# Attention layer: five of a slot's sixteen pair sums folded by VectorE, three batches of ones products instead of four

## The chip, the core and the metric

One NeuronCore of one Trainium2 chip runs the whole program as one launch. The metric is device time in microseconds (us) from start to end of an execution. TensorE (PE) multiplies matrices into PSUM, VectorE (DVE), ScalarE (ACT) and GpSimd (POOL) work on tensors, and SyncE (SP) issues the DMAs. Each has a queue of instructions in a fixed order and waits on semaphores.

## What is computed

Two layers on a tensor of 4 images, 128 channels and 64x64 places. The change touches the first, self-attention over the 4096 places of an image with four heads of 32 channels, an output projection, the residual and a layer norm:

```python
Q = split_heads(x_flat @ Wq + bq); K = ...; V = ...
attn = softmax(einsum('bhnd,bhmd->bhnm', Q, K) * scale, axis=-1)
out = einsum('bhnm,bhmd->bhnd', attn, V)
y = (out.transpose(0, 2, 1, 3).reshape(B, H*W, C) @ Wo + bo) + x_flat
y = (y - mean(y)) / sqrt(var(y) + EPS) * gamma + beta
```

The second layer (a 3x3 convolution, a spectral mix and a Mamba scan) is the same in both kernels.

## The kernel before

**Slots and quads.** The attention runs in 128 slots: 4 images x 4 heads x 8 chunks of 512 queries. A slot has 32 key tiles of 128 keys, taken four at a time in 8 quads (`v` = 0 to 7). In each quad TensorE alternates four score products of queries by keys for the slot two ahead (`max_tile`, L369), of which VectorE takes the row maximum (L569), and four products of keys by queries for this slot (`exp_tile`, L376), of which ScalarE takes the exponential (L493). Behind these eight stands one batch of four products of exponentials and values (`attn_v`, L387), for the quad before; the four lie side by side in 32-column groups of the array. The trace shows each fp32 product as two records, so a batch is 8 records.

**The softmax denominator.** GpSimd adds the two halves of each pair of exponential tiles (L560, 16 pair sums of 128x512 a slot, in a ring `sums` of 8). TensorE then multiplies them by ones (`sum_exps`, L399), four pair sums a batch: a batch each for pairs 0 to 3, 4 to 7, 8 to 11 and 12 to 15, behind the exponentials of quads 2, 4, 6 and of quad 0 of the next slot. VectorE copies the result from PSUM (`read_den`, L580) in quad 0 of the next slot.

**Rings.** The score products that VectorE reads share three PSUM banks (`d` ring), those that ScalarE reads three others (`a` ring). A product can be issued only when the reader has released the bank of three products earlier. With four tiles in a quad, the fourth maximum product waits for VectorE's first maximum of the same quad. The exponentials go to `exps`, 4 buffers of one pair each.

**Around it.** After the first maximum of a slot's scores is joined (L574), TensorE turns it (`turn_max`, L405) in quad 1 and VectorE writes it as two fp32r rows (`shift_rows`, L586 and L588). In 24 of the slots the queries, keys and values of a chunk of the next image are projected: `project` in quads 1 and 2, ScalarE adds the bias into `full` (L507), VectorE makes its fp32r high part (`high`, L595, quads 2 and 4) and low part (`low`, L599, quads 3 and 5), both in `hilo`, and SyncE stores them. The 8 chunks of the first image are projected before slot 0, in a prologue. In 32 slots a chunk of the output is finished: `spread_den` in quad 4, `join_heads` (L431) in quad 5, `out_proj` in quad 6, `mean` in quad 7, `variance` in quad 1 of the next slot, with `normalise`, `add_x`, `centre` and `scale` on VectorE. ScalarE copies each slot's output into `heads_out`, which stays in SBUF for all four heads of an image (L501). The order is written out by loops over slot and quad, one loop for each engine.

Of the kernel before, what the change touches and what calls it, by code (L numbers as in the profile page):

```python
# [52 lines left out]
NS = B * HEADS * NCH  # L53
PRE = -NCH - 2
NF = B * NCH

# [73 lines left out]
def layer0(nc, x, w, z_ext, nb=B):  # L130
    qk_split = nc.dram_tensor("qk_split", [B, 2, 2, C, L], F32, kind="Internal").ap()
    v_dram = nc.dram_tensor("v_dram", [B, HEADS, 128, NT * D], F32, kind="Internal").ap()
    d_at, a_at = ring_positions()
    with ExitStack() as ctx:
# [22 lines left out]
        v_ring = sb("v_ring", [128, 2, NT, D])  # L157
        exps = sb("exps", [128, 4, 2 * CH])
        sums = sb("sums", [128, 8, CH])
        heads_out = sb("heads_out", [128, HEADS, L])  # L160
        mpart = sb("mpart", [128, 2, 4, NCH])
# [21 lines left out]
        with nc.Block() as block:  # L183
# [33 lines left out]
            def _(act):  # L217
# [6 lines left out]
                             "mneg_ready", "mrow_hi")]  # L224
        (made, split_ready, v_stored, recip_ready, squared, rstd_ready, scale_ready, z_ready, z_stored, f_in) = [
            sem(s) for s in ("made", "split_ready", "v_stored", "recip_ready", "squared", "rstd_ready", "scale_ready", "z_ready",
                             "z_stored", "f_in")]
        q_in = [sem(f"q_in{i}") for i in range(4)]
        k_piece = [sem(f"k_piece{i}") for i in range(NCH)]
        k_in, v_in, x_in, split_stored, mrow_stored, den_stored = [  # L230
            [sem(f"{s}{i}") for i in range(2)] for s in ("k_in", "v_in", "x_in", "split_stored", "mrow_stored", "den_stored")]
        MAX_BANK, EXP_BANK, OUT_BANK, DEN_BANK = 0, 3, 6, 7
# [17 lines left out]
        with nc.Block() as block:  # L250
            @block.sync
            def _(sp):
# [45 lines left out]
                def store_den(n):  # L298
# [6 lines left out]
                    sp.dma_start(denom[row:row + 4, half, :], den_parts[::D, n % 2, :]).then_inc(den_stored[n % 2], 16)  # L305

                def store_max(m):
# [10 lines left out]
                for n in range(PRE, NS + 2):  # L318
# [13 lines left out]
                    if 0 <= n - 1 < NS:  # L332
                        store_den(n - 1)
                    if 0 <= n + 1 < NS:
                        store_max(n + 1)
# [15 lines left out]
            def _(pe):  # L351
# [27 lines left out]
                def attn_v(n, v):  # L379
                    if v == 0:  # L380
                        if n:
                            pe.wait_ge(out_read, n)
                        if n % NCH == 0:
                            pe.wait_ge(v_in[n // NCH % 2], 16 * (n // NCH // 2 + 1))
                    pe.wait_ge(a_done, a_at["exp", n, 4 * v + 3] + 1)
                    for i in range(4):
                        ins = nc.tensor.matmul(ps[D * i:D * i + D, OUT_BANK, :], v_ring[:, n // NCH % 2, 4 * v + i, :],  # L387
                                               exps[:, (2 * v + i // 2) % 4, CH * (i % 2):CH * (i % 2) + CH],
                                               start=(v == 0), stop=(v == QUADS - 1))
                        if i % 2:  # L390
                            ins.then_inc(av_done, 1)

                def sum_exps(n, v):
                    if v == 1 and n:
                        pe.wait_ge(den_read, n)
                    pe.wait_ge(summed, n * PAIRS + 2 * v + 2)
                    for j in range(4):
                        u = 2 * v - 2 + j
                        nc.tensor.matmul(ps[D * j:D * j + D, DEN_BANK, :], ones_d[:, :], sums[:, u % 8, :],  # L399
                                         start=(v == 1), stop=(v == QUADS - 1)).then_inc(sum_used, 1)  # L400

# [25 lines left out]
                def join_heads(f):  # L427
                    pe.wait_ge(out_read, last_slot(f) + 1)
                    d_room(("join", f))
                    for h in range(HEADS):  # L430
                        ins = nc.tensor.matmul(d_bank(("join", f))[D * h:D * h + D, :], sel_o[:, :],  # L431
                                               heads_out[:, h, chunk(f % NCH)], start=True, stop=True)
                    ins.then_inc(d_ready, 1)
# [16 lines left out]
                for n in range(PRE, NS + 2):  # L450
                    p, f, g = projection_at(n), finish_at(n), finish_at(n - 1)
                    for v in range(QUADS):
# [24 lines left out]
                        if f is not None and v == 5:  # L477
                            join_heads(f)
                        if 0 <= m < NS and u % 2:
                            sum_exps(m, u)  # L480

            @block.scalar
            def _(act):
# [3 lines left out]
                def exp_tile(n, t):  # L487
                    u, half = t // 2, t % 2
                    ready(("exp", n, t))
                    if half == 0 and n * PAIRS + u >= 4:  # L490
                        act.wait_ge(av_done, n * PAIRS + u - 3)
                        act.wait_ge(summed, n * PAIRS + u - 3)
                    nc.scalar.activation(exps[:, u % 4, CH * half:CH * half + CH], a_bank(("exp", n, t)), ACT.Exp, scale=SCALE  # L493
                                         ).then_inc(a_done, 1)

                def read_out(n):
                    act.wait_ge(av_done, n * PAIRS + PAIRS)
                    f = batch_of(n) * NCH + n % NCH
                    if n // NCH % HEADS == 0 and f >= NCH:
                        act.wait_ge(d_done, d_at["join", f - NCH] + 1)  # L500
                    nc.scalar.copy(heads_out[:, n // NCH % HEADS, chunk(n % NCH)], ps[:, OUT_BANK, :]).then_inc(out_read, 1)  # L501

                def add_bias(p, i):
                    ready(("proj", p, i))
                    if p:
                        act.wait_ge(split_ready, 2 * p + i - 1)
                    nc.scalar.activation(full[:, i, :], a_bank(("proj", p, i)), ACT.Identity, bias=bias[:, i:i + 1]).then_inc(a_done, 1)  # L507

# [44 lines left out]
            @block.gpsimd  # L553
            def _(pool):
                for n in range(NS):
                    for u in range(PAIRS):
                        pool.wait_ge(a_done, a_at["exp", n, 2 * u + 1] + 1)
                        if n * PAIRS + u >= 8:
                            pool.wait_ge(sum_used, n * PAIRS + u - 7)
                        pool.tensor_tensor(sums[:, u % 8, :], exps[:, u % 4, 0:CH], exps[:, u % 4, CH:2 * CH], ALU.add).then_inc(summed, 1)  # L560

            @block.vector
            def _(dve):
# [12 lines left out]
                def read_den(n):  # L576
                    dve.wait_ge(sum_used, n * PAIRS + PAIRS)
                    if n >= 2:
# [11 lines left out]

                def high(p, i):
                    dve.wait_ge(a_done, a_at["proj", p, i] + 1)
                    if p >= 2:
                        dve.wait_ge(split_stored[p % 2], 64 * (p // 2))
                    nc.vector.tensor_copy(hilo[:, p % 2, i, 0, :], full[:, i, :]).then_inc(made, 1)  # L595

                def low(p, i):
                    dve.wait_ge(made, 2 * p + i + 1)
                    nc.vector.tensor_tensor(hilo[:, p % 2, i, 1, :], full[:, i, :], hilo[:, p % 2, i, 0, :].bitcast(F32), ALU.subtract  # L599
                                            ).then_inc(split_ready, 1)  # L600

# [33 lines left out]
                for n in range(PRE, NS + 2):  # L635
                    p, f, g = projection_at(n), finish_at(n), finish_at(n - 1)
                    for v in range(QUADS):
                        for m, t in max_tiles(n, v):
                            max_tile(m, t)
                        if v == 0:  # L640
                            if 0 <= n + 1 < NS:
                                join_max(n + 1)
                            if 0 <= n - 1 < NS:
                                read_den(n - 1)
                        if v == 1 and 0 <= n + 1 < NS:
                            shift_rows(n + 1)
                        if p is not None:
                            if v in (2, 4):
                                high(p, v // 2 - 1)
                            if v in (3, 5):  # L650
                                low(p, v // 2 - 1)
                            if v == 6:
# [667 lines left out]
```

## Time and profile before

| | us |
|---|---|
| median of 3 runs (lowest, highest) | 5985.74 (5984.24, 5988.39) |
| the profiled execution | 5988.07 |
| its span, first to last instruction | 5986.3 |
| TensorE busy | 5515.8 (92%) |
| VectorE busy | 4841.2 (81%) |
| GpSimd busy | 4207.8 (70%) |
| ScalarE busy | 3701.3 (62%) |

The profile gives each engine's busy time, groups of instructions by line, and a timeline in order of time. The first layer fills the first 3950 us or so. "Idle" in brackets is the time an engine stood still ahead of an instruction, with the engine that ended it. A busy TensorE is modelled from pipelined matmuls: it is in the distance between starts that its pace is read.

### The profile page before, as it was taken

What the parts mean: (1) busy time and instruction counts of PE and PEld (TensorE: products, weight loads), DVE (VectorE), ACT (ScalarE), POOL (GpSimd) and SP (SyncE); (2) the same over time, 40 slices, a digit from 0 to 9 for tenths busy, and PEclk for the clock granted to TensorE, in tenths of its full rate; (3) what the DMA queues carried; (4) which work ended last, traced back from release to release, by engine and by line L of the source; (5) the groups of instructions that cost most, each with busy time, mean ns of one, the idle gap of its engine ahead of it and who ended that gap; (6) DMA issues with size and microseconds to landing.
All of it is one profiled execution on the core that took longest, in us unless ns stands there. A gap on an engine that the chain in (4) does not pass through costs nothing. (4 is left out here: it accounts for less than half of the span.)

```text
span 5986.3 us, 84041 instructions
## 1 busy us (share of the span) xinstructions
PE 5515.8 (92%) x27184; PEld 2520.1 (42%) x27184; DVE 4841.2 (81%) x7122; ACT 3701.3 (62%) x7290; POOL 4207.8 (70%) x3213
## 2 busy tenths in 40 slices
PE   7999999999999999999999999968888878888887
PEld 4444444444444444444444444423333333333333
DVE  7777777777777777777777777639999999999999
ACT  3666666665666666666666666656666666666665
POOL 2767666677676677776667776638787887878787
PEclk8999999999999999999999999989999999999999
DMA  4011010110110101101010000024444444454444
GB/s 135 21 43 41 20 38 22 43 40 27 43 35 21 45 20 43 41 24 36 24 26 22 8 22 13 20 94 172 168 161 168 160 169 162 168 168 160 168 160 153
DMA packets 292503, 464.74 MB, mean 78 GB/s; under 512 B 72384, under 2 KB 95808, under 8 KB 290624
## 3 DMA queue, kind: packets, MB, share of 16 engines
q1 hardware_dynamic: 292064, 459.37, 23.6%
q8 instruction: 217, 3.56, 0.2%
q14 instruction: 222, 1.82, 0.1%
HBM read 381.41 MB, written 76.28 MB: 76 GB/s over the span
## 5 line engine op out<-in xcount | busy, mean ns | idle before, releaser
L560 POOL TENSOR_TENSOR sums<-exps 128x512 f32<-128x512 f32 x2048 | 2617.2, 1298 | 1313.2 <-ACT exps L493 1308.3
L569 DVE TENSOR_REDUCE mpart<-ps 128x1 f32<-128x512 f32 x4096 | 2541.6, 683 | 818.9 <-PE ps L369 818.9
L493 ACT ACTIVATE exps<-ps 128x512 f32<-128x512 f32 x4096 | 2127.9, 603 | 1404.0 <-PE ps L376 1403.6
L369 PE MATMUL ps<-k_st,q_ring 96*128 96x512 f32 x4096 | 1753.9, 429 | 17.3 <-DMA k_st<-qk_split 8.9
L1232 POOL TENSOR_TENSOR hc<-hh,c_rep 128x512 f32<-128x512 f32 x1024 | 1361.8, 1338 | 392.3 <-DVE hh L1195 391.9
L376 PE MATMUL ps<-q_ring,k_st 98*128 98x512 f32 x4096 | 1621.7, 397 | 4.0 <-ACT exps L493 3.6
L1195 DVE TENSOR_TENSOR_SCAN hh<-d_a,carry,ps 128x512 f32<-128x512 f32 x1024 | 1308.6, 1281 | 1.0
L369 PEld LDWEIGHTS ps<-k_st,q_ring 96*128 96x128 f32 x4096 | 775.1, 189 | 1063.4 <-DVE mpart L569 508.2
L387 PE MATMUL ps<-exps,v_ring 128*32 128x512 f32 x8192 | 1090.8, 605 | 0.0
L376 PEld LDWEIGHTS ps<-q_ring,k_st 98*128 98x128 f32 x4096 | 777.7, 190 | 148.4 <-ACT exps L493 17.3
L1021 PE MATMUL ps<-s_u,sel_g 128*128 128x512 f32 x1024 | 559.1, 549 | 199.0 <-DVE hh L1195 197.4
L1119 ACT ACTIVATE d_a<-d_a,a_neg 128x512 f32<-128x512 f32 x1024 | 730.8, 720 | 3.6 <-DMA d_a<-dt_dram 2.0
L1181 DVE TENSOR_TENSOR ps<-ps,b_rep 128x512 f32<-128x512 f32 x1024 | 700.8, 687 | 12.6 <-PE ps L1021 11.6
L1021 PEld LDWEIGHTS ps<-s_u,sel_g 128*128 128x128 f32 x1024 | 194.7, 191 | 870.0 <-DVE hh L1195 752.8
L399 PE MATMUL ps<-sums,ones_d 128*32 128x512 f32 x4096 | 533.1, 592 | 0.0
L1004 PE MATMUL ps<-hc,sel_y 128*32 128x512 f32 x2048 | 287.2, 633 | 183.6 <-DVE yt L1166 114.7
L387 PEld LDWEIGHTS ps<-exps,v_ring 128*32 128x32 f32 x8192 | 161.2, 108 | 416.9 <-ACT exps L493 361.2
L1112 ACT COPY carry<-hh 128x1 f32<-128x1 f32 x1024 | 186.7, 183 | 238.8 <-DVE hh L1195 238.5
L939 PE MATMUL ps<-za,wtap 128*128 128x512 f32 x528 | 266.0, 598 | 27.2 <-DMA stage_j<-z_ext 27.2
L986 PE MATMUL ps<-zp,wconv 128*128 128x512 f32 x576 | 290.0, 604 | 0.0
L399 PEld LDWEIGHTS ps<-sums,ones_d 128*32 128x32 f32 x4096 | 133.0, 110 | 306.6 <-issue 298.1
L1064 ACT CAST s_u<-ux 64x1024 fp32r<-64x1024 f32 x66 | 68.9, 1045 | 286.0 <-POOL ux L1223 285.2
(106 smaller groups left out, 3075.4 us busy)
## 6 DMA issues: line engine op xcount, KB each, us to landing
d_a<-dt_dram SPq DMA_DIRECT2D x1040, 256.0 KB
qk_split<-hilo SPq DMA_DIRECT2D x128, 256.0 KB, 2.3
q_ring<-qk_split SPq DMA_DIRECT2D x384, 64.0 KB, 2.0
k_st<-qk_split SPq DMA_DIRECT2D x45, 512.0 KB, 7.1
dt_dram<-dt SPq DMA_DIRECT2D x33, 512.0 KB, 2.8
za<-z_ext SPq DMA_DIRECT2D x33, 320.0 KB, 3.8
zp<-z_ext SPq DMA_DIRECT2D x32, 320.0 KB, 6.6
xc<-in_x SPq DMA_DIRECT2D x32, 256.0 KB, 3.0
```

Source lines behind the costliest of these rows:

```text
L369: nc.tensor.matmul(d_bank(("max", m, t)), q_ring[0:PARTS, m % 4, 128 * i:128 * i + 128], k_st[0:PARTS, g % 2, chunk(kc)], start=True, stop ...
L376: nc.tensor.matmul(a_bank(("exp", n, t)), k_st[0:SHIFT, n // NCH % 2, 128 * t:128 * t + 128], q_ring[0:SHIFT, n % 4, :], start=True, stop= ...
L387: ins = nc.tensor.matmul(ps[D * i:D * i + D, OUT_BANK, :], v_ring[:, n // NCH % 2, 4 * v + i, :], exps[:, (2 * v + i // 2) % 4, CH * (i % ...
L399: nc.tensor.matmul(ps[D * j:D * j + D, DEN_BANK, :], ones_d[:, :], sums[:, u % 8, :], start=(v == 1), stop=(v == QUADS - 1)).then_inc(sum_ ...
L493: nc.scalar.activation(exps[:, u % 4, CH * half:CH * half + CH], a_bank(("exp", n, t)), ACT.Exp, scale=SCALE).then_inc(a_done, 1)
L560: pool.tensor_tensor(sums[:, u % 8, :], exps[:, u % 4, 0:CH], exps[:, u % 4, CH:2 * CH], ALU.add).then_inc(summed, 1)
L569: nc.vector.tensor_reduce(mpart[:, m % 2, t % 4, t // 4:t // 4 + 1], d_bank(("max", m, t)), AX.X, ALU.max).then_inc(d_done, 1)
L1021: nc.tensor.matmul(ps[:, U_BANK + g % NU, :], sel_g[:, j, :], s_u[:, p, s, :], start=True, stop=True).then_inc(u_rep, 1)
L1119: nc.scalar.activation(d_a[:, g % NDA, :], d_a[:, g % NDA, :], ACT.Exp, scale=a_neg[:, s * 8 + j:s * 8 + j + 1]).then_inc(da_ready, 1)
L1181: nc.vector.tensor_tensor(bu, bu, b_rep[:, p, :], ALU.mult).then_inc(bu_ready, 1)
L1195: nc.vector.tensor_tensor_scan(hh[:, g % NHH, :], d_a[:, g % NDA, :], ps[:, U_BANK + g % NU, :], carry[:, it % STEPS, s * 8 + j:s * 8 + j ...
L1232: pool.tensor_tensor(hc[:, g % NHC, :], hh[:, g % NHH, :], c_rep[:, p, :], ALU.mult).then_inc(hc_ready, 1)
```

## The change

GpSimd writes the pair sums 0 to 4 of a slot to a new tile `held` of five buffers, not to the ring. VectorE adds these five into `held_sum` in four pieces of 128 columns, one behind the maxima of each of quads 3 to 6 (`join_held`): each piece reads 5 x 128 elements per partition in the order column by column, so that consecutive elements lie 512 elements apart, and writes 128. TensorE multiplies by ones in three batches: pairs 5 to 8 in quad 5, 9 to 12 in quad 7, and 13 to 15 with `held_sum` in quad 0 of the next slot.

It also moves other work. `exps` has 8 buffers, not 4. To make room, `heads_out` goes: ScalarE copies a slot's output to one of two buffers `out_sb`, SyncE stores each (256 KB) to DRAM (`store_out`) and, for each of the 32 finished chunks, loads the four heads back (1 MB, `load_heads`) before `join_heads`. The high part of a projection is written by a second ScalarE activation and the low part by GpSimd, so VectorE has neither. `read_den` moves from quad 0 to quad 1 behind `shift_rows`. `h_in`, `joined` and `out_stored` are semaphores.

```diff
+EXPS = 8
+HELD = 5
+ALONE = PAIRS - HELD
+UNITS = ALONE + 1
+def units(u):
+    return {4: (5, 6, 7, 8), 6: (9, 10, 11, 12), 7: (13, 14, 15, None)}.get(u, ())
...
 def store_out(n):
+    sp.wait_ge(out_read, n + 1)
+    f = batch_of(n) * NCH + n % NCH
+    if f >= 2 * NCH:
+        sp.wait_ge(h_in, 16 * (f - 2 * NCH + 1))
+    sp.dma_start(out_dram[...], out_sb[:, n % 2, :]).then_inc(out_stored[n % 2], 16)
+def load_heads(f):
+    if f:
+        sp.wait_ge(d_ready, d_at["join", f - 1] + 1)
+    sp.wait_ge(out_stored[f % 2], 16 * (last_slot(f) // 2 + 1))
+    sp.dma_start(heads_in[:, :, :], out_dram[...]).then_inc(h_in, 16)
...
 def sum_exps(n, v):
-    if v == 1 and n:
+    if v == 4 and n:
         pe.wait_ge(den_read, n)
-    pe.wait_ge(summed, n * PAIRS + 2 * v + 2)
-    for j in range(4):
+    pe.wait_ge(summed, n * PAIRS + (2 * v + 1 if v < 7 else PAIRS))
+    for j, u in enumerate(units(v)):
+        if u is None:
+            pe.wait_ge(joined, 4 * n + 4)
...
 def join_heads(f):
-    pe.wait_ge(out_read, last_slot(f) + 1)
+    pe.wait_ge(h_in, 16 * f + 16)
...
 # ScalarE, add_bias: a second activation
+    nc.scalar.activation(hilo[:, p % 2, i, 0, :], a_bank(("proj", p, i)), ACT.Identity, bias=bias[:, i:i + 1]).then_inc(a_done, 1)
 # GpSimd, behind the pair sums of quads 2 and 4
+def low(p, i):
+    pool.wait_ge(a_done, a_at["proj", p, i] + 1)
+    pool.tensor_tensor(hilo[:, p % 2, i, 1, :], full[:, i, :], hilo[:, p % 2, i, 0, :].bitcast(F32), ALU.subtract)
 # VectorE
+def join_held(n, i):
+    if i == 0:
+        dve.wait_ge(summed, n * PAIRS + HELD)
+        if n:
+            dve.wait_ge(sum_used, n * UNITS)
+    a = slice(128 * i, 128 * i + 128)
+    nc.vector.tensor_reduce(held_sum[:, a], held[:, :, a].rearrange("p k c -> p c k"), AX.X, ALU.add).then_inc(joined, 1)
```

VectorE in one slot with neither a projection nor a finish, before (from the joining of the maxima to the end of the slot's maxima; line numbers are those of each kernel):

```order
L574 TENSOR_REDUCE mneg<-mpart 128x4
L580 COPY den_parts<-ps 128x512
L569 TENSOR_REDUCE mpart<-ps 128x1 x4
L586 CAST mrow<-ps 4x128
L588 TENSOR_TENSOR mrow<-ps,mrow 4x128
L569 TENSOR_REDUCE mpart<-ps 128x1 x28
```

The same stretch in the changed kernel:

```order
L630 TENSOR_REDUCE mneg<-mpart 128x4
L625 TENSOR_REDUCE mpart<-ps 128x1 x4
L642 CAST mrow<-ps 4x128
L644 TENSOR_TENSOR mrow<-ps,mrow 4x128
L636 COPY den_parts<-ps 128x512
L625 TENSOR_REDUCE mpart<-ps 128x1 x8
L654 TENSOR_REDUCE held_sum<-held 128x128
L625 TENSOR_REDUCE mpart<-ps 128x1 x4
L654 TENSOR_REDUCE held_sum<-held 128x128
```

The copy of the denominators now stands behind the two row instructions, and a piece of the held sum stands between each two groups of four maxima from quad 3 on; two more pieces follow in the same way.

SyncE's queue in a slot that finishes a chunk, in the changed kernel:

```order
L269 DMA q_ring<-qk_split 32x512 x3
L359 DMA x_f<-in_x 128x512
L326 DMA out_dram<-out_sb 128x512
L319 DMA denom<-den_parts 4x512
L333 DMA heads_in<-out_dram 128x4x512
L338 DMA q_ring<-mrow 1x4x128 x2
L343 DMA z_ext<-z_sb 128x512
```

The third and the fifth row are new; the rows with `mrow`, which the exponentials of the next slot wait for, now stand behind the wait of the fifth.

## Rows read from the trace of the kernel before

**Rows 1.** The page: span, busy time of each engine.
```profile
span 5986.3 us, 84041 instructions
PE 5515.8 (92%) x27184; PEld 2520.1 (42%) x27184; DVE 4841.2 (81%) x7122; ACT 3701.3 (62%) x7290; POOL 4207.8 (70%) x3213
```

**Rows 2.** Windows, steady first layer: length, busy per engine, granted clock, DMA share.
```profile
1000.00:2000.00 1000.00, 1000.00 (x5540) 479.38 (x5537) 740.68 (x1261) 611.70 (x1157) 675.51 (x527) 1.00 0.12 34
```

**Rows 3.** TensorE timeline, quads 1 to 3: start us, length us, line.
```profile
1503.25 0.50 PE L369 MATMUL ps<-k_st,q_ring 96*128 96x512 f32 x1
...
1504.81 0.50 PE L369 MATMUL ps<-k_st,q_ring 96*128 96x512 f32 x1
1505.15 0.40 PE L376 MATMUL ps<-q_ring,k_st 98*128 98x512 f32 x1
...
1506.69 0.50 PE L369 MATMUL ps<-k_st,q_ring 96*128 96x512 f32 x1
...
1508.21 0.40 PE L369 MATMUL ps<-k_st,q_ring 96*128 96x512 f32 x1
1508.44 0.39 PE L376 MATMUL ps<-q_ring,k_st 98*128 98x512 f32 x1
...
1510.61 0.50 PE L369 MATMUL ps<-k_st,q_ring 96*128 96x512 f32 x1
...
1513.68 0.50 PE L369 MATMUL ps<-k_st,q_ring 96*128 96x512 f32 x1
```

**Rows 4.** Lines, window 1000 to 2000: count, busy, mean ns, idle before, releaser.
```profile
L560 POOL TENSOR_TENSOR sums<-exps 128x512 f32<-128x512 f32 x527 | 676.3, 1304 | 322.8 <-ACT exps L493 321.3
L569 DVE TENSOR_REDUCE mpart<-ps 128x1 f32<-128x512 f32 x1054 | 654.1, 683 | 212.8 <-PE ps L369 212.8
L399 PE MATMUL ps<-sums,ones_d 128*32 128x512 f32 x1052 | 137.0, 592 | 0.0
L633 DVE TENSOR_TENSOR scaled<-centred,rstd 128x512 f32<-128x512 f32 x8 | 7.6, 946 | 0.0
L574 DVE TENSOR_REDUCE mneg<-mpart 128x4 f32<-128x32 f32 x33 | 5.9, 178 | 0.0
```

**Rows 5.** VectorE timeline of the same slot, with idle before and its releaser.
```profile
1503.46 0.69 DVE L580 COPY den_parts<-ps 128x512 f32<-128x512 f32 x1 [1.04 <-PE ps L399]
1504.07 2.47 DVE L569 TENSOR_REDUCE mpart<-ps 128x1 f32<-128x512 f32 x4
1506.46 0.27 DVE L586 CAST mrow<-ps 4x128 fp32r<-4x128 f32 x1
1506.76 0.28 DVE L588 TENSOR_TENSOR mrow<-ps,mrow 4x128 fp32r<-4x128 f32 x1
...
1514.22 2.48 DVE L569 TENSOR_REDUCE mpart<-ps 128x1 f32<-128x512 f32 x4 [0.58 <-PE ps L369]
```

**Rows 6.** VectorE timeline in the prologue.
```profile
48.78 4.87 DVE L569 TENSOR_REDUCE mpart<-ps 128x1 f32<-128x512 f32 x8
53.55 0.42 DVE L595 CAST hilo<-full 128x512 fp32r<-128x512 f32 x1
...
55.68 0.68 DVE L606 TENSOR_TENSOR v_stage<-ps,bv_sb 128x512 f32<-128x512 f32 x1
56.28 4.87 DVE L569 TENSOR_REDUCE mpart<-ps 128x1 f32<-128x512 f32 x8
```

**Rows 7.** TensorE timeline at the end of the first layer.
```profile
3931.61 1.06 PE L399 MATMUL ps<-sums,ones_d 128*32 128x512 f32 x8
...
3936.68 1.94 PE L431 MATMUL ps<-heads_out,sel_o 128*32 128x512 f32 x8
```

**Rows 8.** DMA issues: count, KB each, median us from issue to landing.
```profile
qk_split<-hilo SPq DMA_DIRECT2D x128, 256.0 KB, 2.3
k_st<-qk_split SPq DMA_DIRECT2D x45, 512.0 KB, 7.1
v_ring<-v_dram SPq DMA_DIRECT2D x16, 512.0 KB, 3.8
```

More of the change, by code:

```diff
@@ L157, in layer0 @@
         v_ring = sb("v_ring", [128, 2, NT, D])
-        exps = sb("exps", [128, 4, 2 * CH])
+        exps = sb("exps", [128, EXPS, 2 * CH])
         sums = sb("sums", [128, 8, CH])
-        heads_out = sb("heads_out", [128, HEADS, L])
+        held = sb("held", [128, HELD, CH])
+        held_sum = sb("held_sum", [128, CH])
+        out_sb = sb("out_sb", [128, 2, CH])
+        heads_in = sb("heads_in", [128, HEADS, CH])
         mpart = sb("mpart", [128, 2, 4, NCH])
@@ L332, in _ @@
                     if 0 <= n - 1 < NS:
+                        store_out(n - 1)
                         store_den(n - 1)
+                    if f is not None:
+                        load_heads(f)
                     if 0 <= n + 1 < NS:
@@ L489, in exp_tile @@
                     ready(("exp", n, t))
[L490 to L493, printed above, removed]
+                    if half == 0 and n * PAIRS + u >= EXPS:
+                        act.wait_ge(av_done, n * PAIRS + u - EXPS + 1)
+                        act.wait_ge(summed, n * PAIRS + u - EXPS + 1)
+                    nc.scalar.activation(exps[:, u % EXPS, CH * half:CH * half + CH], a_bank(("exp", n, t)), ACT.Exp, scale=SCALE
                                          ).then_inc(a_done, 1)
@@ L497, in read_out @@
                     act.wait_ge(av_done, n * PAIRS + PAIRS)
[L498 to L501, printed above, removed]
+                    if n >= 2:
+                        act.wait_ge(out_stored[n % 2], 16 * (n // 2))
+                    nc.scalar.copy(out_sb[:, n % 2, :], ps[:, OUT_BANK, :]).then_inc(out_read, 1)
                 def add_bias(p, i):
@@ L554, in _, with pair_sum @@
             def _(pool):
[L555 to L560, printed above, removed]
+                def pair_sum(n, u):
+                    pool.wait_ge(a_done, a_at["exp", n, 2 * u + 1] + 1)
+                    if u < HELD:
+                        if n:
+                            pool.wait_ge(joined, 4 * n)
+                        dst = held[:, u, :]
+                    else:
+                        i = n * ALONE + u - HELD
+                        if i >= 8:
+                            pool.wait_ge(sum_used, (i - 8) // ALONE * UNITS + (i - 8) % ALONE + 1)
+                        dst = sums[:, i % 8, :]
+                    pool.tensor_tensor(dst, exps[:, u % EXPS, 0:CH], exps[:, u % EXPS, CH:2 * CH], ALU.add).then_inc(summed, 1)
+                def low(p, i):
+                    pool.wait_ge(a_done, a_at["proj", p, i] + 1)
+                    pool.tensor_tensor(hilo[:, p % 2, i, 1, :], full[:, i, :], hilo[:, p % 2, i, 0, :].bitcast(F32), ALU.subtract
+                                       ).then_inc(split_ready, 1)
+                for n in range(PRE, NS):
+                    p = projection_at(n)
+                    for v in range(QUADS):
+                        if 0 <= n:
+                            pair_sum(n, 2 * v)
+                            pair_sum(n, 2 * v + 1)
+                        if p is not None and v in (2, 4):
+                            low(p, v // 2 - 1)
             @block.vector
@@ L589, in shift_rows @@
                                             ALU.subtract).then_inc(d_done, 1)
[L591 to L600, printed above, removed]
+                def join_held(n, i):
+                    if i == 0:
+                        dve.wait_ge(summed, n * PAIRS + HELD)
+                        if n:
+                            dve.wait_ge(sum_used, n * UNITS)
+                    a = slice(128 * i, 128 * i + 128)
+                    nc.vector.tensor_reduce(held_sum[:, a], held[:, :, a].rearrange("p k c -> p c k"), AX.X, ALU.add).then_inc(joined, 1)
                 def values(p):
@@ L642, in _ @@
                                 join_max(n + 1)
+                        if v == 1:
+                            if 0 <= n + 1 < NS:
+                                shift_rows(n + 1)
                             if 0 <= n - 1 < NS:
                                 read_den(n - 1)
-                        if v == 1 and 0 <= n + 1 < NS:
-                            shift_rows(n + 1)
+                        if v in (3, 4, 5, 6) and 0 <= n < NS:
+                            join_held(n, v - 3)
                         if p is not None:
[L648 to L651, printed above, removed]
                             if v == 6:
```

36 lines of the change are left out of this document (23 added, 13 removed).

## The prediction

> **What bounds the kernel now.** I read the page first: TensorE is busy 92% of the span, VectorE 81% [rows 1]. A share over the whole span mixes two layers, so I then asked for a window inside the first layer: there TensorE is busy 1000 of 1000 us at a granted clock of 1.00, the 2.4 GHz level, VectorE 741, GpSimd 676, ScalarE 612 [rows 2]. So TensorE sets the pace, and what leaves its queue shortens the slot, if nobody else becomes late. The modelled busy time can't be used as a price: the group of ones products shows 137.0 us busy for 1052 records [rows 4], though its batches overlap with others. The price is read from the distance between starts.
>
> The TensorE timeline gives it [rows 3]. A quad that holds eight score products, a batch of values and a batch of ones takes 1510.61 - 1506.69 = 3.92 us. The next, without the batch of ones, takes 1513.68 - 1510.61 = 3.07 us. A batch of ones is worth **0.85 us**.
>
> How near is VectorE? In an undisturbed quad it starts its first maximum 0.54 us behind TensorE's first product (1514.22 against 1513.68), works 2.48 us and had stood idle 0.58 us before [rows 3, 5]. In quads with a batch of ones that gap is 0.85 us larger, 1.43. So in a short quad VectorE has 0.58 us to spare, less than one 128x512 instruction. What a late VectorE costs is seen in quad 1: its copy of the denominators waits 1.04 us for TensorE, and its first maximum starts at 1504.07, 0.82 us behind TensorE's 1503.25, so 0.28 late [rows 3, 5]. TensorE's fourth maximum product then starts 1.56 us into the quad, not 1.52, and the product behind it 0.34 later, not 0.23: together 0.15 us lost [rows 3]. From this one point I take: **loss = lateness - 0.13 us**, nothing below that.
>
> **Part 1, the batch of ones.** One of four batches goes from each of 128 slots: 128 x 0.85 = **108.8 us** off TensorE's path. The other three are only moved. None of their waits should bind: the batch in quad 5 needs nine pair sums where the one in quad 6 needed twelve; GpSimd's two sums take 2 x 1.30 = 2.6 us of a quad of 3.07 [rows 4], and `exps` with 8 buffers lets it lag further than before. The held sum is needed in quad 0 of the next slot, a quad after its last piece.
>
> **Part 2, the four pieces on VectorE.** This is the term on which the result turns. No row shows a reduction with five inputs lying apart. The near rows: the reduction of 512 elements takes 683 ns, that of 32 elements 178 ns [rows 4], so (683 - 178)/480 = 1.05 ns an element and 145 ns fixed. A piece of 640 elements is then 0.145 + 640 x 1.05 = **0.82 us**. The upper bound is the slowest row per element: 946 ns for 512 elements with two SBUF inputs [rows 4] is 1.56 ns an element, or 1.15 us a piece; and if each hop took two steps for one, 0.145 + 640 x 2.10 = 1.49 us. Below, nothing faster than 0.82 is seen for a reduction, and as VectorE is not the bound a faster piece would gain at most the few hundredths below. I take 0.82, since both neighbours are reductions and one of them reads SBUF.
>
> The Trainium skill speaks on both sides here (Vector Engine (DVE) Microarchitecture Reference, section 5.2, Measured stream behaviour on trn2): a program with two sources of which one hops on every element ran at 1.73 ns a column and not 1.05, while a one-source program alternating between two distant regions kept the full rate. By the first a piece would be some 1.25 us, an estimate, and the slot would lose more than the batch gives; by the second it is the 0.82 that I take. No row here reads in that order.
>
> What a piece of P us does: neighbours on VectorE overlap by 0.08 us (1503.46 + 0.69 against 1504.07, [rows 5]), so a piece put between two groups shifts the next group by P - 0.16, of which 0.58 was idle. Lateness after a short quad is x = P - 0.74. For 0.82, x = 0.08. The pieces stand in quads 3 to 6. Quads 3, 4 and 6 are now short; quad 5 has a batch and absorbs it all. Into quad 4 VectorE comes 0.08 late, into quad 5 0.16, of which 0.03 is lost; into quad 6 not late; into quad 7 0.08. Total lost: **0.03 us a slot**. In general, past x = 0.13, it is (x - 0.13) + x + (x - 0.13) = 3x - 0.26.
>
> **Part 3, the copy of the denominators.** Moved behind the row instructions it no longer waits for TensorE; the 0.15 us of quad 1 come back. But now it delays quad 2: quad 1 is 3.44 us with the loss [rows 3], 3.29 without. VectorE: first maximum at 0.54, the cast 2.39 later (1506.46 - 1504.07), the second row instruction 0.30 later and 0.28 long, then the copy's 0.61: next group at about 4.08, where 3.29 + 0.54 = 3.83 would be in time. Lateness 0.25, loss 0.12. With part 2 nothing is left of the 0.15, except in the 24 slots with a projection and the 31 behind a finish, whose quad 1 holds one product more: 55 x 0.12 = 6.6. I take **5 us** gained in all for parts 2 and 3 (from -5 to 15).
>
> **Part 4, the high and low parts.** In the steady slots VectorE loses them where it had room; ScalarE's second activation and GpSimd's subtraction (1.3 us, as its pair sums) stand in slots whose quads 1 and 2 are longer, and ScalarE is 61% busy. Costed at nothing; if a projection bank were released late, 0.5 us x 24 = 12 us. In the prologue it counts: there VectorE works without a rest, in stretches of eight maxima and a projection. The period is 56.28 - 48.78 = 7.50 us, of which 55.68 - 53.55 = 2.13 are high and low parts [rows 6]. Five such periods stand in the trace: 10.7 us. Against it, the first chunks go through GpSimd (1.3 against 0.7 us) and the loop of store and reload may become the limit. I take **8 us** gained, from 0 to 11.
>
> **Part 5, the outputs by way of DRAM.** 256 KB more out per slot and 1 MB back per finished chunk, beside a DMA share of 0.12 [rows 2]. The store lands in about 2.3 us, as that of `hilo`; 1 MB takes twice the 3.8 us of `v_ring`, 7.6 us, or twice the 7.1 of `k_st`, 14.2 [rows 8]. ScalarE's copy is done some 3.5 us into the slot, SyncE's denominator store waits until about 7.5, so the load is issued there and lands at 15 (22 at the slow price). `join_heads` stands behind five quads, at about 21 us. Hidden. Queued behind the load's wait on SyncE are the maxima rows, needed only at the next slot. At the very end nothing hides it: the last batch of ones starts at 3931.61 and `join_heads` at 3936.68 [rows 7]; now it is 3931.6 + 0.8 for the copy + 2.3 + 7.6 = 3942.3. **5 us** lost (3 to 12).
>
> **Sum.** 108.8 + 5 + 8 - 5 = 116.8 us gained. The profiled execution of 5988.07 would be 5871.3; it lies 2.3 above the median of 5985.74, against which runs are compared, so I predict **5869 us**.
>
> **Rival A: the strided read is slow, and VectorE becomes the bound.** The ring of three banks makes TensorE wait in quads 4, 5 and 7. Before the pieces a slot gains 0.85 + 0.15 - 0.12 = 0.88 us; 3x - 0.26 eats that at x = 0.38, a piece of 1.12 us. For a price I take the middle between the row-bound 1.15 and the doubled 1.49, 1.32 us: x = 0.58, 1.48 lost, 0.60 x 128 = 77 us slower, less 3 for parts 4 and 5: **6060 us**. For it: five addresses 2 KB apart are unlike anything in this trace. Against it: the reductions pay the same fixed part and step whether from PSUM or SBUF. Chance 0.14. The first of the two measurements that the Trainium skill gives (same page and section) falls on this side, with its estimate of 1.25 us a piece.
>
> **Rival B: half-way.** A piece between 0.95 and 1.12 us: 3x - 0.26 is 0.37 at 0.95 and 0.88 at 1.12. At 1.02 us, 0.58 lost against 0.88: 38 us, with 3 more **5945 us**. Chance 0.08.
>
> **Rival C: the heads come late.** If 1 MB moves at `k_st`'s price or slower behind other loads, `join_heads` waits, say 2 us in each of 32 slots (22 + landing against 21): 64 us given back, **5933 us**. For it: nothing of 1 MB is loaded now. Against: a DMA share of 0.12. Chance 0.07.
>
> **How the numbers follow.** Forecast 0.71, with its own spread of 5855 to 5885 from the bounds of parts 3 to 5. A measurement of this kernel can tell about 0.2%, 12 us. Forecast, B and C are faster; of A a small part lies within 12 us. Faster 0.84, same 0.03, slower 0.13. For 8 in 10 the range takes the forecast and most of B and C: 5850 to 5950.
>
> **What would show it.** In the trace after: quads 3, 4 and 6 at 3.07 us and quad 5 at 3.92 mean part 2 right; the mean of the `held_sum` reductions near 820 ns; under rival A it is above 1.1 us and quads 4, 5 and 7 stretch, with TensorE's loads released by the maxima. A plain slot, now 4 x 3.92 + 3 x 3.07 + 3.44 = 28.3 us, should be near 27.4. `join_heads` with idle before it released by a DMA would be rival C. The first exponential should come some 8 us earlier than before, and the last `join_heads` some 10 us behind the last batch of ones. The forecast fails if the piece is priced wrong, since all the rest is small.

## The result

The changed kernel takes **6005.79 us** (median of 7 runs, 6001.62 to 6008.31), the kernel before 5986.65 (7 runs). The ratio is 1.0032, 95% interval 1.0020 to 1.0044: slower by a third of a per cent, 19 us. Forecast were 5869 us, faster by 2%. The profiled execution took 6005.80 us, its span is 6004.0.

The page of the changed kernel, span, busy times and costliest groups of VectorE and GpSimd:

```profile
span 6004.0 us, 82923 instructions
PE 5470.6 (91%) x26160; PEld 2464.0 (41%) x26160; DVE 5350.3 (89%) x7506; ACT 3768.8 (63%) x7354; POOL 4272.5 (71%) x3277
...
L625 DVE TENSOR_REDUCE mpart<-ps 128x1 f32<-128x512 f32 x4096 | 2536.0, 679 | 487.2 <-PE ps L400 476.9
...
L654 DVE TENSOR_REDUCE held_sum<-held 128x128 f32<-128x640 f32 x512 | 666.9, 1303 | 3.6 <-POOL held L602 3.6
```

Against [rows 1], TensorE's busy time falls by 45 us and VectorE's rises by 509: 667 of pieces, less 82 of high and low parts that it lost (31.6 and 50.6 us in the kernel before) and smaller differences that were not taken apart. The new row is the one to look at: a piece takes **1303 ns**, not the 820 that the forecast took. The maxima are unchanged at 0.68 us [rows 4], but VectorE's idle time ahead of them is 487 us, where before it was 819. The same group on the page of the kernel before:

```profile
L569 DVE TENSOR_REDUCE mpart<-ps 128x1 f32<-128x512 f32 x4096 | 2541.6, 683 | 818.9 <-PE ps L369 818.9
```

What TensorE does with that is in its timeline, quad 4 of a slot in the steady part (start, length, idle before with its releaser):

```profile
1519.57 0.50 PE L400 MATMUL ps<-k_st,q_ring 96*128 96x512 f32 x1
...
1521.38 0.50 PE L400 MATMUL ps<-k_st,q_ring 96*128 96x512 f32 x1 [0.15 <-DVE mpart L625]
1521.72 0.39 PE L407 MATMUL ps<-q_ring,k_st 98*128 98x512 f32 x1
...
1523.04 0.50 PE L400 MATMUL ps<-k_st,q_ring 96*128 96x512 f32 x1
```

and quads 5, 6 and 7 of the slot before it:

```profile
1494.27 0.50 PE L400 MATMUL ps<-k_st,q_ring 96*128 96x512 f32 x1
...
1496.22 0.50 PE L400 MATMUL ps<-k_st,q_ring 96*128 96x512 f32 x1 [0.28 <-DVE mpart L625]
...
1498.75 0.50 PE L400 MATMUL ps<-k_st,q_ring 96*128 96x512 f32 x1
...
1501.81 0.50 PE L400 MATMUL ps<-k_st,q_ring 96*128 96x512 f32 x1
...
1503.63 0.50 PE L400 MATMUL ps<-k_st,q_ring 96*128 96x512 f32 x1
...
1506.15 0.50 PE L400 MATMUL ps<-k_st,q_ring 96*128 96x512 f32 x1
```

The fourth maximum product of quad 4 starts 1.81 us into the quad, in quad 5 1.95, in quad 7 1.82, where an undisturbed quad has 1.52 [rows 3]: VectorE has not released the bank. Quad 4 takes 3.47 us (3.07 undisturbed), quad 5 4.48 (3.92), quad 7 4.34 (3.92). VectorE's side of quads 3 and 4 (the slot of the first timeline), without a pause once the first piece has begun:

```profile
1517.04 2.48 DVE L625 TENSOR_REDUCE mpart<-ps 128x1 f32<-128x512 f32 x4 [0.47 <-PE ps L400]
1519.44 1.29 DVE L654 TENSOR_REDUCE held_sum<-held 128x128 f32<-128x640 f32 x1
1520.65 2.46 DVE L625 TENSOR_REDUCE mpart<-ps 128x1 f32<-128x512 f32 x4
1523.05 1.31 DVE L654 TENSOR_REDUCE held_sum<-held 128x128 f32<-128x640 f32 x1
```

A slot with neither projection nor finish (a plain slot, 72 of the 128) takes 28.8 us (28.3 before): the batch gives 0.85 back and the three quads take 1.38. Slots with a projection or a finish, whose quads are longer, come out shorter than they were (by the distances of starts 31.1 from 31.2, and 32.6 from 33.1 in those behind and with a finish), which is why the whole is only 19 us slower.

### The profile page after: what moved, and what is told of

Read it like the earlier page. It is cut to its first block and busy times, and to the rows that moved or that the text cites. A ratio compares the mean times of both kernels' runs of the same rounds, so it can differ in the third digit from the quotient of the medians.

```text
span 6004.0 us, 82923 instructions
## 1 busy us (share of the span) xinstructions
PE 5470.6 (91%) x26160; PEld 2464.0 (41%) x26160; DVE 5350.3 (89%) x7506; ACT 3768.8 (63%) x7354; POOL 4272.5 (71%) x3277
## 5 line engine op out<-in xcount | busy, mean ns | idle before, releaser
L526 ACT ACTIVATE exps<-ps 128x512 f32<-128x512 f32 x4096 | 2159.0, 601 | 1366.3 <-PE ps L407 1364.4
L602 POOL TENSOR_TENSOR sums<-exps 128x512 f32<-128x512 f32 x1408 | 1801.0, 1290 | 633.8 <-ACT exps L526 619.5
L400 PE MATMUL ps<-k_st,q_ring 96*128 96x512 f32 x4096 | 1782.7, 436 | 79.1 <-DVE mpart L625 52.5
L602 POOL TENSOR_TENSOR held<-exps 128x512 f32<-128x512 f32 x640 | 807.2, 1278 | 570.3 <-ACT exps L526 570.3
L654 DVE TENSOR_REDUCE held_sum<-held 128x128 f32<-128x640 f32 x512 | 666.9, 1303 | 3.6 <-POOL held L602 3.6
L432 PE MATMUL ps<-sums,ones_d 128*32 128x512 f32 x2816 | 399.0, 592 | 0.0
```

The costliest lines, as they stand in the source:

```text
L400: nc.tensor.matmul(d_bank(("max", m, t)), q_ring[0:PARTS, m % 4, 128 * i:128 * i + 128], k_st[0:PARTS, g % 2, chunk(kc)], start=True, stop ...
L526: nc.scalar.activation(exps[:, u % EXPS, CH * half:CH * half + CH], a_bank(("exp", n, t)), ACT.Exp, scale=SCALE).then_inc(a_done, 1)
L602: pool.tensor_tensor(dst, exps[:, u % EXPS, 0:CH], exps[:, u % EXPS, CH:2 * CH], ALU.add).then_inc(summed, 1)
L654: nc.vector.tensor_reduce(held_sum[:, a], held[:, :, a].rearrange("p k c -> p c k"), AX.X, ALU.add).then_inc(joined, 1)
```

## The experiments

The question is why a piece takes 1.30 us, and whether that alone is what turned the result. Theory 1: reading with a hop of 512 elements at every element is slow. Rival 2: a reduction pays for each group of five. Rival 3: VectorE is slowed by GpSimd beside it. And beside all of them: some other edit of the change ate the gain. Ratios are against the kernel before, run with them on the same chip. The diffs show the line that matters; where a piece fills fewer or more columns than 128, `held_sum` is sized for it and set to 1.0 at the start.

**e1, the same reduction read side by side.**

```diff
-nc.vector.tensor_reduce(held_sum[:, a], held[:, :, a].rearrange("p k c -> p c k"), AX.X, ALU.add)
+flat = held[:, :, :].rearrange("p k c -> p (k c)")[:, 640 * i:640 * i + 640]
+nc.vector.tensor_reduce(held_sum[:, a], flat.rearrange("p (c k) -> p c k", k=HELD), AX.X, ALU.add)
```

> The changed kernel, but each piece reads 640 elements of `held` that lie side by side (128 groups of five neighbours), so what it adds is not the five pair sums; count, groups and time of issue are unchanged. Theory 1 (reading with a hop of 512 elements at every element is what costs): the piece falls from 1305 ns to about 820 ns, the quads 4, 5 and 7 fall back to 3.07, 3.92 and 3.92 us, the plain slot from 28.8 to 27.5 us, and the time to about 5873 us. Rival 2 (a reduction pays for each of its 128 groups of five): the piece stays at 1.3 us and the time at 6006. Rival 3 (reading SBUF beside GpSimd slows it): the same, 1.3 us and 6006.

Measured: 5857.13 us, ratio 0.9784 (0.9769 to 0.9798), with this row:

```profile
L655 DVE TENSOR_REDUCE held_sum<-held 128x128 f32<-128x640 f32 x512 | 413.0, 807 | 3.6 <-POOL held L602 3.6
```

The same count, groups and neighbours at 807 ns. Rivals 2 and 3 fall: it is the order of reading. And 149 us hang on it (6005.8 - 5857.1).

**e2, four additions in the place of the pieces.**

```diff
-nc.vector.tensor_reduce(held_sum[:, a], held[:, :, a].rearrange("p k c -> p c k"), AX.X, ALU.add)
+if i: dve.wait_ge(joined, 4 * n + i)
+nc.vector.tensor_tensor(held_sum[:, :], held_sum[:, :] if i else held[:, 0, :], held[:, i + 1, :], ALU.add)
```

> The changed kernel with the four pieces replaced by four additions of 128x512 (held 0 + held 1, then each of the others), one behind the maxima of quads 3 to 6; the sum is the same. Each has two inputs in SBUF. By the rows of before such an operation takes 690 ns alone and 790 to 820 beside GpSimd, so lateness is 0.08 us or less: about 5873 us, range 5862 to 5890. Rival 3 (contention with GpSimd is the cost): each addition above 1.0 us, GpSimd's pair sums above 1.4 us, time above 5920.

Measured: 5857.00 us, ratio 0.9782 (0.9768 to 0.9797).

```profile
L602 POOL TENSOR_TENSOR sums<-exps 128x512 f32<-128x512 f32 x1408 | 2017.5, 1452 | 300.6 <-ACT exps L526 272.9
L602 POOL TENSOR_TENSOR held<-exps 128x512 f32<-128x512 f32 x640 | 807.4, 1278 | 537.9 <-ACT exps L526 537.9
L655 DVE TENSOR_TENSOR held_sum<-held_sum,held 128x512 f32<-128x512 f32 x384 | 303.8, 791 | 0.1
```

The additions take 0.79 us, as expected (the row has three of a slot's four; all four average 0.80). Here the contention is seen, on the other side: GpSimd's sums into `sums`, of which most run beside an addition, rise to 1452 ns on average (1290 in the change), those of `held`, of which none does, stay at 1278. GpSimd had room for it. The kernel computes what the reference does and is 2.2% faster than before.

**e3, the hop after every pair.**

```diff
-nc.vector.tensor_reduce(held_sum[:, a], held[:, :, a].rearrange("p k c -> p c k"), AX.X, ALU.add)
+nc.vector.tensor_reduce(held_sum[:, 128 * i:128 * i + 64], held[:, :, a].rearrange("p k (c t) -> p c k t", t=2), AX.XY, ALU.add)
```

> The changed kernel, but each piece reads the same 640 elements in pairs of neighbours, hopping 512 elements after each pair, and adds ten elements into each of 64 results; the other 64 columns of the held sum are constant. Theory 1 in the form 'only a lone element between hops costs' (the pair rule of the Trainium skill, Vector Engine (DVE) Microarchitecture Reference, section 5.2): 0.8 us a piece and about 5873 us. Theory 1 in the form 'each hop costs alike': half the hops, about 1.06 us a piece, and about 5930 us. Rival 3: 1.3 us and 6006.

Measured: 5855.45 us, ratio 0.9780 (0.9764 to 0.9797).

```profile
L655 DVE TENSOR_REDUCE held_sum<-held 128x64 f32<-128x640 f32 x512 | 413.1, 807 | 3.6 <-POOL held L603 3.6
```

807 ns with half the hops, as side by side: among five places, hops cost nothing once two neighbours are read after each. This is what the Trainium skill says of pairs (Vector Engine (DVE) Microarchitecture Reference, section 5.2), and the trace agrees. What is slow is a lone element between two hops, in a way that e5 narrows.

**e4, no pieces.** `join_held` and the waits on `joined` taken out, a constant tile multiplied in its place.

```diff
-if v in (3, 4, 5, 6) and 0 <= n < NS:
-    join_held(n, v - 3)
```

> The changed kernel without the four pieces: VectorE adds nothing, and TensorE multiplies a constant tile in the place of the held sum; everything else as changed. This is the change with the piece at no cost. Theory 1: quads 4, 5 and 7 at 3.07, 3.92 and 3.92 us, plain slot 27.4 us, about 5869 us. If other edits of the change (outputs by way of DRAM, low parts on GpSimd) had taken the gain, it would stay above 5950.

Measured: 5855.10 us, ratio 0.9780 (0.9766 to 0.9795). VectorE works 748 of 1000 us here, 838 in e1, and both kernels take the same time:

```profile
1000.00:2000.00 1000.00, 1000.00 (x5469) 490.45 (x5466) 747.79 (x1275) 643.73 (x1218) 709.93 (x562) 1.00 0.19 56
```

```profile
1000.00:2000.00 1000.00, 1000.00 (x5466) 487.45 (x5462) 837.97 (x1410) 643.49 (x1219) 709.54 (x562) 1.00 0.19 56
```

(first e4, then e1; columns as in [rows 2]). So a piece of 0.81 us is hidden (the 2 us between e1 and e4 lie within the spread of their runs), no other edit took the gain, and the slow pieces cost 6005.8 - 5855.1 = 150.7 us.

**e5, two places.** The reduction alternates between two pair sums.

```diff
-nc.vector.tensor_reduce(held_sum[:, a], held[:, :, a].rearrange("p k c -> p c k"), AX.X, ALU.add)
+nc.vector.tensor_reduce(held_sum[:, 320 * i:320 * i + 320], held[:, 0:2, 40 * i:40 * i + 320].rearrange("p k c -> p c k"), AX.X, ALU.add)
```

> The changed kernel, but each piece adds the first two pair sums only, 320 columns of them: 640 elements read as before, alternating between two places 512 elements apart at every element, into 320 results; the other three pair sums are left out. Theory 1 as 'a lone element between two hops is slow, wherever it hops': 1.3 us a piece as in the change, 6006 us. The other form, from the Trainium skill (Vector Engine (DVE) Microarchitecture Reference, section 5.2: a one-source stream alternating between two regions at the full rate): 0.81 us a piece, 5857 us.

Measured: 5861.07 us (2 runs), ratio 0.9791 (0.9771 to 0.9810).

```profile
L655 DVE TENSOR_REDUCE held_sum<-held 128x320 f32<-128x640 f32 x512 | 422.4, 826 | 3.7 <-POOL held L603 3.7
```

My form of theory 1 falls: between two places even lone elements come at nearly the full rate (826 ns where side by side takes 807). The Trainium skill's second measurement (same page and section) agrees with this row; it is one for two places.

**e6, the hop given to the writer.** `held` is laid out with the five sums of a column side by side. GpSimd writes with a step of five elements.

```diff
-held = sb("held", [128, HELD, CH])
+held = sb("held", [128, CH, HELD])
...
-dst = held[:, u, :]
+dst = held[:, :, u]
...
-nc.vector.tensor_reduce(held_sum[:, a], held[:, :, a].rearrange("p k c -> p c k"), AX.X, ALU.add)
+nc.vector.tensor_reduce(held_sum[:, a], held[:, a, :], AX.X, ALU.add)
```

> The changed kernel with `held` laid out column by column, five pair sums side by side: GpSimd writes with a step of five elements, VectorE's pieces read side by side and give the same sum. If the hop costs only the engine that reads: pieces 0.81 us, GpSimd's sums 1.28 us as now, 5857 us. If GpSimd's writes pay as VectorE's reads did (0.75 ns an element, 1.66 us each): the five are 0.4 us longer, GpSimd lags by 1 us over the first quads and the 8 buffers take it up, still below 5870. If they cost double (2.6 us each), GpSimd needs 27.2 us of a slot of 27.4 and the time rises above 5880.

Measured: 5855.03 us, ratio 0.9780 (0.9766 to 0.9795).

```profile
L602 POOL TENSOR_TENSOR held<-exps 128x512 f32<-128x512 f32 x640 | 816.0, 1296 | 529.9 <-ACT exps L526 529.9
L654 DVE TENSOR_REDUCE held_sum<-held 128x128 f32<-128x640 f32 x512 | 412.3, 806 | 3.7 <-POOL held L602 3.7
```

GpSimd pays 18 ns for writing apart (1278 in the change, 1296 here). The same sum as the change, at 5855 us: with e2 the version to keep.

**e7, the prologue.** e2 with the low parts of the prologue back on VectorE.

```diff
+if n < 0 and v in (2, 4):      # VectorE
+    low(p, v // 2 - 1)
...
-if p is not None and v in (2, 4):      # GpSimd
+if p is not None and n >= 0 and v in (2, 4):
```

> The kernel with four additions in the place of the pieces, and in the prologue alone the low parts back on VectorE (0.69 us each, where GpSimd takes 1.26); the high parts stay on ScalarE. If the prologue of the change is held by the loop of store and reload, in which the low part stands, a shorter low part brings the first exponential forward by 3 to 6 us, to some 87 us and 5853 in all. If it is held by the loads alone, nothing changes: 5857 us.

Measured: 5853.98 us, ratio 0.9779 (0.9764 to 0.9793), not distinct from e2. The first exponential product starts at 91.6 us, as in e2 (the row has the first and the last start in us):

```profile
L407 PE MATMUL ps<-q_ring,k_st x4096: 389/395/796, 91.6 to 3792.6; 98*128 98x512 f32 x196
```

So a shorter low part brings nothing. TensorE's waits in the prologue of the changed kernel name the reloads of `k_st` (total us, times, longest us):

```profile
PE ps L400 <- DMA k_st<-qk_split: 14.2, 6, 5.5
PEld ps L400 <- DMA k_st<-qk_split: 9.8, 5, 3.7
```

In the kernel before, over the same 110 us, TensorE waits 14.2 us for these reloads (24.0 in the changed kernel) and 12.5 us for VectorE's copy of the values, `v_stage` (1.7 in the changed kernel). Waits for VectorE fell there by 11 us, those for the reloads rose by 10.

**e8, a piece of 96 columns.**

```diff
-nc.vector.tensor_reduce(held_sum[:, a], held[:, :, a].rearrange("p k c -> p c k"), AX.X, ALU.add)
+a = slice(96 * i, 96 * i + 96)
+nc.vector.tensor_reduce(held_sum[:, a], held[:, :, a].rearrange("p k c -> p c k"), AX.X, ALU.add)
```

> The changed kernel, reading with hops as it does, but each piece adds 96 columns of five and not 128; the last 128 columns of the held sum are constant. A piece should take 0.145 + 480 x 1.81 ns = 1.01 us, x = 0.27. By the rule of the prediction, 3x - 0.26 = 0.56 us lost in a plain slot; the full pieces lost 1.39 where the rule gives 1.43, and 150.7 us in all where 128 slots of 1.39 would be 178, so I expect 0.56 x 128 x 0.85 = 61 us over the kernel without pieces: about 5916 us. If there were no threshold (loss in proportion to lateness): 150.7 x 0.27 / 0.56 = 73 us, 5928. If only the slot's total of VectorE work counted, there would be no loss at all, since VectorE then is busy well below TensorE: 5857 us.

Measured: 5907.18 us, ratio 0.9868 (0.9852 to 0.9885).

```profile
L656 DVE TENSOR_REDUCE held_sum<-held 128x96 f32<-128x480 f32 x512 | 518.0, 1012 | 3.6 <-POOL held L603 3.6
```

The piece is 1.01 us as expected, the loss 52 us where the rule with its threshold gave 61 and proportion 73. A plain slot takes 27.9 us, 0.50 more than in e1, where the rule says 0.56 and proportion 0.67. VectorE's total did not decide: it works 854 of 1000 us, 16 more than in e1, and 50 us are lost.

**e9, four places, and e12, three.** As e5, with `held[:, 0:4, ...]` in 160 columns and `held[:, 0:3, ...]` in 213.

```diff
-nc.vector.tensor_reduce(held_sum[:, a], held[:, :, a].rearrange("p k c -> p c k"), AX.X, ALU.add)
+nc.vector.tensor_reduce(held_sum[:, 160 * i:160 * i + 160], held[:, 0:4, 40 * i:40 * i + 160].rearrange("p k c -> p c k"), AX.X, ALU.add)
```

> The changed kernel, but each piece adds the first four pair sums only, 160 columns of them: 640 elements, hopping among four places 512 elements apart, into 160 results; the fifth pair sum is left out. With two places a piece took 826 ns, with five 1303. If any number of places above two is slow: 1.3 us and about 6005 us. If the cost grows with the places (a row of two free, five 0.48 us dearer): between, about 1.14 us and 5955 us. If only five is slow: 0.82 us and 5858 us.

> The changed kernel, but each piece adds the first three pair sums only, 213 columns of them: 639 elements, hopping among three places; the other two pair sums are left out. Two places took 826 ns, four 1305, five 1303. If every number above two is slow: 1.30 us a piece and about 6005 us. If the step lies above three: 0.82 us and 5858 us.

Measured: four places 6006.37 us, ratio 1.0034 (1.0020 to 1.0047); three places 5870.69 us (2 runs), ratio 0.9799 (0.9771 to 0.9828). First the row of e9, then that of e12:

```profile
L655 DVE TENSOR_REDUCE held_sum<-held 128x160 f32<-128x640 f32 x512 | 667.6, 1305 | 3.6 <-POOL held L603 3.6
```

```profile
L655 DVE TENSOR_REDUCE held_sum<-held 128x213 f32<-128x639 f32 x512 | 451.2, 882 | 3.6 <-POOL held L603 3.6
```

So 826, 882, 1305 and 1303 ns for two, three, four and five places. The cost doesn't grow evenly with the places; nearly all of it comes between three and four. "Slow above two" is refuted; the other expectation of e12 was 0.06 us short on the piece. Its kernel before ran at 5990.65 us beside it, 4.5 more than in the other runs; by the ratio, e12 is at some 5866 us on their scale. Why the step lies there these runs don't tell.

**e10, another distance.**

```diff
-held = sb("held", [128, HELD, CH])
+held = sb("held", [128, HELD, CH + 4])
...
-dst = held[:, u, :]
+dst = held[:, u, 0:CH]
```

> The changed kernel with `held` padded: its five buffers lie 516 elements apart, not 512, the sum is the same. If it is the distance of a power of two (2048 bytes) that costs, a piece falls to about 0.81 us and the time to 5857 us. If it is the lone element between hops at whatever distance: 1.30 us and 6006 us, as the change.

Measured: 6014.23 us, ratio 1.0047 (1.0031 to 1.0063), the piece 1327 ns. That the distance is a power of two, 2048 bytes, is not the cause; at 2064 a piece is 24 ns dearer. Larger and smaller distances were not tried.

**e11, the slow pieces elsewhere.**

```diff
-if v in (3, 4, 5, 6) and 0 <= n < NS:
-    join_held(n, v - 3)
+if v in (3, 5, 6, 7) and 0 <= n < NS:
+    join_held(n, (3, 5, 6, 7).index(v))
```

> The changed kernel with its slow pieces as they are, but behind the maxima of quads 3, 5, 6 and 7, not 3, 4, 5 and 6. A piece of 1.30 us shifts the next group by 1.14 us; a quad with a batch of ones has 1.43 us idle and takes that up, a short quad 0.58. So the pieces of quads 5 and 7 are free, those of 3 and 6 cost TensorE 0.41 us each: 0.82 us a plain slot where the change loses 1.39. Scaled from its 150.7 us: 89 us over the kernel without pieces, about 5944 us. If VectorE's total work counted and not its place, nothing would change: 6006 us.

Measured: 5952.80 us, ratio 0.9946 (0.9929 to 0.9963): 53 us faster than the change with the same four pieces of the same length.

```profile
1505.08 1.30 DVE L654 TENSOR_REDUCE held_sum<-held 128x128 f32<-128x640 f32 x1
1506.59 2.48 DVE L625 TENSOR_REDUCE mpart<-ps 128x1 f32<-128x512 f32 x4 [0.21 <-PE ps L400]
1509.00 1.29 DVE L654 TENSOR_REDUCE held_sum<-held 128x128 f32<-128x640 f32 x1
1510.21 2.47 DVE L625 TENSOR_REDUCE mpart<-ps 128x1 f32<-128x512 f32 x4
```

Behind the piece of quad 5 (the first row) VectorE still stands idle 0.21 us; behind that of quad 6 it has no rest. In plain slots quad 5 is back at 3.92 us, from 4.48 in the change, while quads 4 and 7 stay at 3.49 and 4.34; the slot takes 28.25 us, 0.84 over e1, where I expected 0.82. Even a slow piece is free where a batch of ones gives it the time. The cost over the kernel without pieces is 98 us, where I expected 89.

## Why the prediction was wrong, point by point

**What bounds the kernel: right.** TensorE's queue did, and a batch of ones is worth what the quads said: with pieces of 0.81 us or none the plain slot is 27.4 us, as forecast, from 28.3.

**Part 1: right.** None of the moved batches waited for GpSimd or the held sum.

**Part 2: the step that failed.** It is the price of a piece, and through it the 0.03 us that a slot was to lose: a piece takes 1.303 us and the plain slot loses 1.4, 150.7 us in all, more than the batch gives back. The duration of 0.82 us was taken from two reductions that both read side by side. The slope of 1.05 ns an element held for e1 (807 ns). With five places it is (1303 - 145)/640 = 1.81 ns. The forecast had prices on both sides of that (1.15, the slowest row per element, was too low; 1.49, two steps for each hop, too high) and chose the value by the nearest kind of instruction, when what was new in the piece was not its kind but its order of reading, of which the trace had no row. The rival had 0.14. The Trainium skill's page named in the prediction had a measurement for each side, which was worth nearer to even chances; the estimate of 1.25 us from the first of them came close. And the range stopped at 5950, short of the rival's 6060, so it left out the one case that mattered.

**The rule of lateness: right, with a size.** It said that slow pieces cost 3x - 0.26 us a plain slot. At 1303 ns, x = 0.56, that is 1.43; measured 28.8 - 27.4 = 1.4, and quad by quad 0.40, 0.56 and 0.42 where the rule has 0.43, 0.56 and 0.43. Rival A, the mechanism that came, was priced for a piece of 1.32 us at 6060; with 1.30 it came out at 6006. Of the 54 us between, 39 are on the pieces, 1.48 x 128 = 189 against 150.7: some 6 for the 0.02 us of the piece, the rest mainly the other 56 slots, whose quads are longer by a product of a projection or a finish and take part of the lateness up (a slot behind and with a finish loses 0.8, one with a projection 1.1). I had multiplied by 128 what holds for 72. The other 15 are on the kernel under the pieces: by the terms of Rival A it would take 5870 without them, e4 takes 5855. The point from which the change loses, 1.12 us, was for both reasons too low: between the rows for 1012 and 1303 ns below, the time of the kernel before, 5986, is reached at some 1.24 us, an estimate.

| kernel | piece, ns | time, us |
|---|---|---|
| e4 no pieces | - | 5855.1 |
| e6 side by side, e1 | 806, 807 | 5855.0, 5857.1 |
| e5 two places | 826 | 5861.1 |
| e12 three places | 882 | 5870.7 |
| e8 96 columns | 1012 | 5907.2 |
| the change | 1303 | 6005.8 |
| e10 padded | 1327 | 6014.2 |

Nearly flat up to 0.83; between 1012 and 1303 ns 99 us, so some 340 us for each us of the piece: near 3 for a slot, as the rule has it.

**Part 3: right in kind, not tested apart.** The changed kernel's TensorE timeline, the first products of quads 1, 2 and 3:

```profile
1510.06 0.50 PE L400 MATMUL ps<-k_st,q_ring 96*128 96x512 f32 x1
...
1513.23 0.50 PE L400 MATMUL ps<-k_st,q_ring 96*128 96x512 f32 x1
...
1516.50 0.50 PE L400 MATMUL ps<-k_st,q_ring 96*128 96x512 f32 x1
```

Quad 1 fell from 3.44 [rows 3] to 3.17 us and quad 2 is 3.27 where 3.07 is undisturbed: the exchange that I described, 0.07 gained a plain slot where I had 0.03. Both sides were too small. I had the loss of quad 1 at 0.15 and the quad at 3.29 without it. What I left out is the turning product behind the last exponential product, first before, then changed:

```profile
1505.15 0.40 PE L376 MATMUL ps<-q_ring,k_st 98*128 98x512 f32 x1
1505.50 0.27 PE L405 MATMUL ps<-id_sb,mneg 128*4 128x128 f32 x1
```

```profile
1511.80 0.39 PE L407 MATMUL ps<-q_ring,k_st 98*128 98x512 f32 x1
1512.03 0.27 PE L438 MATMUL ps<-id_sb,mneg 128*4 128x128 f32 x1
```

It starts 0.35 us behind that product, and 0.23 in the changed kernel: 0.12 more, together the 0.27 by which quad 1 fell.

**Part 4: wrong, 8 us too good.** The first exponential product starts at 92.4 us, no earlier than before. VectorE now rests in the prologue, but TensorE waits for the reloads of `k_st` in its place (the waits stand under e7). I had named that loop and taken off 2 to 3 us for it and GpSimd's slower low part; it took all. e7 shows that the low part is not what holds it. What else in the loop does stays open.

**Part 5: right, 2 us too dear.** In the profiled execution `join_heads` waits for its load once, at the very end:

```profile
its engine sat idle before it (us, times) until:
  DMA heads_in<-out_dram: 2.9, 1
```

The page gives 5.2 us from the load's issue to its landing, where I had 7.6. The end of the layer on TensorE:

```profile
3946.11 0.61 PE L432 MATMUL ps<-sums,ones_d 128*32 128x512 f32 x3
...
3954.35 1.93 PE L464 MATMUL ps<-heads_in,sel_o 128*32 128x512 f32 x8 [2.93 <-DMA heads_in<-out_dram]
```

From the last batch of ones to `join_heads` it is now 3954.35 - 3946.11 = 8.2 us, before 3936.68 - 3931.61 = 5.1 [rows 7]: 3 us more, where I had said 5, from 3 to 12. Rival C did not come.

**The sum without the failed step.** 5869 forecast, 5855 to 5857 measured with a piece at the forecast length. That the forecast came so near was in part luck: the prologue did not give its 8 us, and the slots gave some 20 more than I had. By the distances of starts in e1, the 27 slots behind and with a finish fell from 33.1 to 31.8 us, the 22 with a projection alone from 31.2 to 30.0, so 1.3 and 1.2 us each where a batch is worth 0.85. In both kinds 0.27 of it stands in quad 1 (4.13 us from 4.40), where the copy no longer holds TensorE; I had given such slots 0.12. In the first kind another 0.2 stands in quads 6 and 7 together (8.85 from 9.04), whose cause stays open.

## What to carry to other kernels

When a price rests on the nearest row, ask in which respect the new instruction differs from it; a difference in access order is a difference in price, and a layout that lets the slow reader read side by side can be had from the writer (here GpSimd paid 18 ns for it). Work added to an engine that is a quarter idle is free only where the idle time lies: the same four pieces cost 98 us in one placing and 151 in another, and pieces of 0.81 us, which fit nearly all into the gap of a quad, cost nothing that the runs can tell. Count the kinds of a repeated stage before multiplying a loss by their number.

## What the runs showed of the hardware

- A VectorE sum (`tensor_reduce`) over 640 fp32 elements in SBUF takes 807 ns when it reads side by side or in pairs that hop, 826 alternating between two places, 882 (639 elements) among three, 1305 among four and 1303 among five, all 2048 bytes apart, and 1327 among five 2064 apart. With the fixed part of 145 ns from [rows 4], an estimate, that is 1.03 to 1.06 ns an element at the fast end and 1.81 at the slow one.
- GpSimd's 128x512 addition writes with a step of 20 bytes at nearly no cost (1296 ns in e6 against 1278).
- VectorE's additions with two SBUF inputs take 0.79 us beside GpSimd and stretch GpSimd's own from 1290 to 1452 ns on average (e2); the reductions don't (1289 in e1, 1288 in e4 without them).
